# An attention block with rotating score slots: the first metric beside the normalisation, a bank per key block, roots on VectorE, closing work spread wider

## The chip, the cores and the metric

One core of a Trainium2 chip runs the whole kernel. The metric is the device time of one execution in microseconds (us), the median of several; lower is better.

## The reference, cut to what matters

The input is 2048 tokens of width 128; there are 16 heads of width 8.

```python
mod = silu(c) @ wmod                                   # six rows of modulation
h = layernorm(x) * (1 + ca) + sa
v = log_map(mu, h)                                     # clip, roots, arccosh, a scaled direction
q, k, vv = v @ Wq.T, v @ Wk.T, v @ Wv.T
g = abs(eta + 0.1 * tanh(tanh((h - mu) @ W1.T + b1) @ W2.T + b2))    # the metric
at = softmax((q * g) @ k.T / sqrt(8))                  # 16 heads, 2048 x 2048 each
x = x + ga * project(project(mu) + 0.1 * (at @ vv) @ Wo.T)
h = layernorm(x) * (1 + cb) + sb
x = x + gb * ((silu(h @ wg.T) * (h @ wu.T)) @ wd.T)    # hidden width 384
```

The kernel never takes a row maximum of the scores. It subtracts from each query a bound, |q| times the largest |k| of the head, which needs the root of |q|^2 * max|k|^2. It is this root that the change moves.

## The kernel before, in words

The queries are cut into four blocks of 512 (`NB`); Bk numbers them. A block has 64 steps j (`STEPS`): four groups of four heads (`NG`, `GH`) times 16 key tiles of 128. In each step TensorE makes the scores of two heads (`score(.., half_=0)`), then the product of probabilities and values of step j-2 (`product`), then the scores of the other two heads. ScalarE takes the exponential of each half step u = 2j or 2j+1, a tile of 128 x 1024, from PSUM into `probs`. There are 128 of these in a block and 512 in all. The scores of a half step go into one of three slots of two PSUM banks each (`slot_bank`), here slot u % 3. Since 128 is not a multiple of 3, the first half steps of a block fall on slots that the last ones of the block before have just used; the waits on `exped` for u < 3 and the order called `early` in steps 1 and 63 (the product goes ahead of the first score) provide for that. The products gather in bank 6 (`O_bank`), which VectorE copies out after every 16 steps (`evacuate`).

Bank 7 (`M_bank`) serves everything else. In block 0 the list `later` puts the values of the key blocks and the metric, query and norm of query blocks 1 to 3 between the score steps, at the steps that `V_AT`, `M1_AT`, `M2_AT`, `Q_AT`, `NQ_AT` name. In blocks 1 to 3 the closing work of the block before (output projection `t_wo`, second normalisation, `t_transpose`, three `t_gate` and `t_up`, four parts of `t_down`) stands at the steps `AT_WO` to `AT_DOWN`. On VectorE `Tail` does its part.

Before block 0 lies a preamble: normalisation and log map in token order, transposes (`metric_T` for h, `v_T` for v), first metric (`metric1`, `metric2`, with `tanh1`, `tanh2` on ScalarE), keys (`k_of`, two PSUM banks in turns), the first queries, squares and norms of the keys (`nk`, `k_max`), the bound of query block 0 (`bound`), and the splitting of keys and queries into three bf16 parts that go through DRAM to get their layout (`store_k`, `load_k`, `load_q`, `load_shift` in SyncE's queue, in this order). The bounds of query blocks 1 to 3 are three ScalarE roots at step 49 of block 0 (`ROOT_AT`). If a check of the sums fails, every engine runs a second pass (`blocks(1)`) with true maxima.

In SyncE's queue one instruction that waits holds up all behind it. In blocks 1 to 3 the order there is: the gathers of groups 0 and 1 (`gather`, 8 transfers each), the store of the block before (waits for `y_ready`, which `tail.result()` gives after the last `t_down`), the reload of x, the gather of group 2.

Of the kernel before, what the change touches and what calls it, by code (L numbers as in the profile page):

```python
# [56 lines left out]
AT_WO, AT_TR, AT_GATE, AT_UP, AT_DOWN = 8, 15, (19, 24, 29), (22, 27, 32), (37, 39, 41, 43)  # L57
# [3 lines left out]
M1_AT, M2_AT, Q_AT, NQ_AT, ROOT_AT = ((7, 10), (21, 24), (35, 38)), (13, 27, 41), (16, 30, 44), (19, 33, 47), 49  # L61
# [17 lines left out]
def build(nc, x, columns, wmod, fixed, w1t, w2t, w_att, wgt, wut, wdt, spread, out):  # L79
    with ExitStack() as ctx:  # L80
# [27 lines left out]
        hs_bf = sb("hs_bf", [P, H], BF16)  # L108
# [24 lines left out]
        def tmp(words, *shape, dt=F32):  # L133
# [5 lines left out]
            if len(shape) == 2:  # L139
# [10 lines left out]
        shift_f = [O_sb[0:H, 0, :], O_sb[0:H, 3, :], x_res[0:H, :, :].rearrange("p a b -> p (a b)"),  # L150
                   h_tm[0:H, 0:TPB, :].rearrange("p a b -> p (a b)")]
# [58 lines left out]
        names = """c_in wmod_in w_in hs_ready ffn_in const_ready pe_mod mod_ready silu_ready ffn_ready  # L210
# [22 lines left out]
        def ring(j):  # L233

            return j % RING if j < STEPS - 1 else 1
# [140 lines left out]
        def _(pool):  # L376
            pool.memset(half[:, :], 0.5).then_inc(S["const_ready"], 1)
            pool.memset(mhalf[:, :], -0.5).then_inc(S["const_ready"], 1)
            pool.memset(V_op[:, :, :], 1.0).then_inc(S["ones_ready"], 1)
            pool.wait_ge(S["const_ready"], 2)  # L380
# [13 lines left out]
            pool.tensor_copy(hs_bf[:, :], hs_sb).then_inc(S["hs_ready"], 1)  # L394
# [24 lines left out]
        def _(act):  # L419
# [29 lines left out]
            for b in range(NB):  # L449
                copy_hT(b)  # L450
# [4 lines left out]
            act.activation(ln_u, u, ACT.Ln).then_inc(S["ln_out"], 1)  # L455

# [5 lines left out]
            def k_split1(b):  # L462
# [3 lines left out]
                act.activation(k_parts[b][:, 0, :], bank(2 + b % 2), ACT.Identity).then_inc(S["k_hi"], 1)  # L466
                act.activation(sqks[b], bank(2 + b % 2), ACT.Square).then_inc(S["k_sq"], 1)
# [5 lines left out]
            def bound(b):  # L473

                if b == 0:
                    act.wait_ge(S["nq_ps"], 1)
                    act.wait_ge(S["kmax_ready"], 1)
                else:
                    act.wait_ge(S["nq_sb"], b)
                act.activation(shift_f[b], bank(6)[0:H, :] if b == 0 else shift_f[b], ACT.Sqrt,  # L480
                               scale=kmax[0:H, NB:NB + 1]).then_inc(S["bound"], 1)

            for m in range(MH):
                tanh1(0, m)
            copy_vT(0)
            copy_vT(1)
            k_split1(0)
            act.wait_ge(S["cols_ps"], 1)
# [888 lines left out]
```

## Time and profile before

| | us |
|---|---|
| median of 3 runs (598.18 to 598.79) | 598.61 |
| profiled execution, span of its instructions | 599.2 |
| profiled execution, its own time | 601.03 |
| TensorE busy / ScalarE busy in the span | 545.6 / 525.6 |
| VectorE busy / GpSimd busy | 143.9 / 23.0 |

The span runs from the first to the last instruction. The busy time of TensorE is that of matmuls, which overlap one another, so 91% does not mean that it does 91% of what it could. The granted clock of TensorE has two levels, 1.2 and 2.4 GHz; its mean over the span was 0.959 of the higher one.

### The profile page before, as it was taken

Reading aid. Unit: us, or ns where it says so; the run is one execution under the profiler, and the core shown is the slowest. Engines: PE = TensorE matmul, PEld = TensorE weight load, DVE = VectorE, ACT = ScalarE, POOL = GpSimd, SP = SyncE. Lnnn points to the kernel's source line nnn. Section 1 sums busy time; section 2 is a strip of 40 time slices with the busy share of each in tenths; the row PEclk is TensorE's granted clock in tenths of the full one; section 3 lists DMA queues with packets and bytes.
Section 4 is the critical chain, followed back from the end, with each engine's and each line's share of the span. In section 5 each row is a group of like instructions: output and inputs, shape, how many; then the busy total and the mean of one; then the engine's idle time right before and its main releaser. Section 6 shows DMA issues by size and latency. Waiting matters only on the chain.

```text
span 599.2 us, 16356 instructions
## 1 busy us (share of the span) xinstructions
PE 545.6 (91%) x7230; PEld 232.9 (39%) x7230; DVE 143.9 (24%) x407; ACT 525.6 (88%) x596; POOL 23.0 (4%) x25
## 2 busy tenths in 40 slices
PE   1566998999979999999999999999999999999855
PEld 0332543554423343345433333454333334553222
DVE  6963303030310251110000711100005211003063
ACT  3564898999999999999999999999999999999811
POOL 2300100000000010000000100000000000000010
PEclk9576999999989999999999999999999999999978
DMA  6012267010040110000100200001000000010000
GB/s 187 4 35 86 94 158 190 8 33 5 29 107 1 46 48 10 3 10 19 29 2 19 74 10 2 5 7 40 7 7 7 4 8 1 11 55 11 1 0 24
DMA packets 13770, 20.90 MB, mean 35 GB/s; under 512 B 2043, under 2 KB 10363, under 8 KB 13411
## 3 DMA queue, kind: packets, MB, share of 16 engines
q1 hardware_dynamic: 12851, 17.48, 11.4%
q0 software_dynamic: 560, 1.97, 0.9%
q8 instruction: 58, 0.95, 0.7%
q10 hardware_dynamic: 288, 0.40, 0.2%
q14 instruction: 13, 0.11, 0.1%
HBM read 13.41 MB, written 4.19 MB: 29 GB/s over the span
## 4 chain that ended last, share of the span: by engine, by line
PE 62%; ACT 17%; issue 8%; DVE 6%; DMA 4%; SPq 1%; POOL 0%; ACTq 0%; DVEq 0%
PE ps L719 26%; PE ps L736 25%; ACT probs L519 14%; PE ps L655 8%; DMA K_op<-k_scr 3%; DVE probs L969 1%; DMA probs<-x_dram 1%; DMA k_scr<-arena 1%; PE ps L624 1%; ACT arena L531 1%; ACT arena L447 1%; SPq L266 1%; PE ps L564 0%; DVE kmax L1038 0%; DVE arena L958 0%
## 5 line engine op out<-in xcount | busy, mean ns | idle before, releaser
L519 ACT ACTIVATE probs<-ps 128x1024 f32<-128x1024 f32 x512 | 481.3, 1121 | 17.0 <-PE ps L719 15.3
L719 PE MATMUL ps<-Q_op,K_op 73*32 73x512 bf16 x4096 | 291.6, 381 | 11.0 <-ACT probs L519 6.7
L736 PE MATMUL ps<-probs,V_op 128*32 128x512 f32 x2048 | 271.7, 595 | 1.3 <-ACT probs L519 0.8
L719 PEld LDWEIGHTS ps<-Q_op,K_op 73*32 73x32 bf16 x4096 | 117.5, 96 | 238.6 <-issue 124.0
L736 PEld LDWEIGHTS ps<-probs,V_op 128*32 128x32 f32 x2048 | 68.8, 111 | 51.3 <-issue 4.9
L1130 DVE COPY O_sb<-ps 128x512 f32<-128x512 f32 x16 | 11.1, 691 | 153.6 <-PE ps L736 153.6
L385 POOL TENSOR_TENSOR small<-small,half 128x4 f32<-128x4 f32 x4 | 5.5, 1383 | 403.3 <-DVE small L1214 403.3
L571 PE MATMUL ps<-fixed_sb,arena 128*128 128x128 f32 x32 | 7.4, 391 | 14.6 <-POOL arena L391 11.1
L1244 DVE SCALAR_TENSOR_TENSOR arena<-arena,ps 128x512 f32<-128x512 f32 x12 | 8.2, 687 | 46.0 <-ACT arena L537 46.0
L1250 DVE TENSOR_TENSOR arena<-ps,arena 128x512 f32<-128x512 f32 x12 | 8.3, 691 | 40.5 <-PE ps L655 40.4
L1264 DVE TENSOR_TENSOR arena<-ps,arena 128x512 f32<-128x512 f32 x3 | 2.1, 691 | 59.9 <-PE ps L655 59.9
L1015 DVE TENSOR_SCALAR arena<-arena,cols 128x512 f32<-128x512 f32 x4 | 1.9, 484 | 60.2 <-ACT arena L438 60.2
L1170 DVE RECIPROCAL arena<-arena 128x512 f32<-128x512 f32 (+1 forms) x4 | 13.4, 3353 | 0.1
L655 PE MATMUL ps<-wd_f,arena 128*32 128x128 f32 x384 | 13.2, 272 | 0.0
L655 PE MATMUL ps<-Q_op,w_sb 128*32 128x512 f32 x96 | 12.6, 592 | 0.0
L655 PE MATMUL ps<-arena,wg_f 128*32 128x512 f32 x96 | 12.5, 593 | 0.0
L655 PE MATMUL ps<-arena,wu_f 128*32 128x512 f32 x96 | 12.5, 592 | 0.0
L655 PEld LDWEIGHTS ps<-wd_f,arena 128*32 128x32 f32 x384 | 11.6, 109 | 2.2 <-issue 0.6
L690 PE MATMUL ps<-ones_bf 128*128 128x512 bf16 x14 | 6.4, 623 | 6.5 <-POOL small L385 6.5
L531 ACT ACTIVATE arena<-ps,mod_cols 128x512 f32<-128x512 f32 x4 | 3.5, 879 | 10.1 <-PE ps L751 10.1
L571 PEld LDWEIGHTS ps<-fixed_sb,arena 128*128 128x128 f32 x32 | 5.3, 198 | 17.6 <-issue 8.4
L537 ACT ACTIVATE arena<-ps 128x512 f32<-128x512 f32 x12 | 8.0, 670 | 3.4 <-PE ps L655 3.4
(167 smaller groups left out, 237.9 us busy)
## 6 DMA issues: line engine op xcount, KB each, us to landing
K_op<-k_scr SPq DMA_DIRECT2D x16, 288.0 KB
Q_op<-q_scr SPq DMA_DIRECT2D x9, 384.0 KB
arena<-O_sb SPq DMA_DIRECT2D x120, 16.0 KB
q_scr<-arena POOLq DMA_DIRECT2D x3, 384.0 KB, 3.0
probs<-x_dram SPq DMA_DIRECT2D x4, 256.0 KB, 4.8
x_res<-x_dram SPq DMA_DIRECT2D x4, 256.0 KB, 3.2
out_dram<-arena SPq DMA_DIRECT2D x4, 256.0 KB, 2.4
Q_op<-q_scr SPq DMA_DIRECT2D x3, 288.0 KB
```

The lines of the kernel that those rows point to most:

```text
L519: act.activation(probs[:, 2 * ring(j) + half_, :], slot_bank(u % 3), ACT.Exp)\
L531: act.activation(h2_T, M_bank, ACT.Identity, scale=mod_cols[:, 0:1], bias=mod_cols[:, 1:2]).then_inc(S["h2T_done"], 1)
L537: act.activation(th[m], from_bank, ACT.Tanh, scale=0.5).then_inc(S["gate_th"], 1)
L571: ins = pe.transpose(bank(b % 2)[:, P * t:P * (t + 1)], src[:, TPB * b + t, :], ident_sb)
L655: ins = pe.matmul(to[CW * c:CW * (c + 1), :], weights[:, CW * c:CW * (c + 1)], moving, start=start, stop=stop, tile_position=(0, CW * c))
L690: ins = pe.matmul(to, ones_bf[:, 0:P], ones_bf[:, 0:BT], start=True, stop=True)
L719: ins = pe.matmul(slot_bank(u % 3)[CW * c:CW * (c + 1), i, :], K_op[0:rows, kt // TPB, h, at_k:at_k + CW], Q_op[0:rows, at_q:at_q + BT], s ...
L736: ins = pe.matmul(O_bank[32 * i:32 * (i + 1), :], V_op[:, kt, VW * h:VW * h + 32], probs[:, 2 * ring(j) + i // 2, BT * (i % 2):BT * (i % 2 ...
L1130: dve.tensor_copy(O_sb[:, g, :], O_bank).then_inc(S["o_evac"], 1)
L1170: c.did(dve.reciprocal(rec_T[rows, :], rec_T[rows, :]))
L1244: dve.scalar_tensor_tensor(gl[m], th[m], 1.0, gates, ALU.add, ALU.mult).then_inc(S["gated"], 1)
L1250: dve.tensor_tensor(hid[:, m, :], ups, gl[m], ALU.mult).then_inc(S["glu_done"], 1)
```

## The change

It does six things. (1) The first metric is computed while the other blocks are still being normalised; ScalarE's list of table loads changes with it. (2) Each of the four key blocks gets a PSUM bank of its own (2 to 5), the four key norms go into the four quarters of one bank, and one reduction over 128 rows and three small copies replace four reductions. (3) A root of nothing on ScalarE (`kmax[:, 7:8]`) ahead of the keys loads the root table early. (4) The bounds of query blocks 1 to 3 are computed on VectorE, by a shift of the bits and one Newton step; the first instruction reads `M_bank` and gives it free. (5) In the first pass slots and `probs` are counted on through all blocks, `early` is gone, and ScalarE's blocks 1 to 3 are written out instead of looped. (6) The closing work stands further apart. Ten matmuls that only keep TensorE busy are put ahead of the first `v_T`, and ten instead of seven ahead of the scores.

```diff
-AT_WO, AT_TR, AT_GATE, AT_UP, AT_DOWN = 8, 15, (19, 24, 29), (22, 27, 32), (37, 39, 41, 43)
+AT_WO, AT_TR, AT_GATE, AT_UP, AT_DOWN = 8, 15, (19, 27, 35), (23, 31, 39), (43, 47, 51, 55)
...
+        def slot(Bk, p, u):
+            return (u + 2 * STEPS * Bk) % 3 if p == 0 else u % 3
+        def early(p, j):
+            return p == 1 and j in (1, STEPS - 1)
+        def ring(Bk, p, j):
+            if p == 0:
+                return (STEPS * Bk + j) % RING
+            return 1 if j == STEPS - 1 else j % RING
...
+            act.activation(kmax[:, 7:8], half[:, 0:1], ACT.Sqrt)
...
-                    if j == ROOT_AT:
-                        bound(b)
...
-                if u >= 3:
+                if u >= 3 or (p == 0 and not start):
                     pe.wait_ge(S["exped"], Bk * 2 * STEPS + u - 2)
...
+            keep_warm(10, bank(5))
             v_T(0)
...
+            def k_max():
+                dve.wait_ge(S["nk_ps"], NB)
+                dve.tensor_reduce(kmax[:, 0:1], bank(0), AX.X, ALU.max).then_inc(S["nk_done"], 1)
+                dve.wait_ge(S["nk_done"], 1)
+                for b in range(1, NB):
+                    vec.did(dve.tensor_copy(kmax[0:H, b:b + 1], kmax[2 * H * b:2 * H * b + H, 0:1]))
+                vec.after()
+                dve.tensor_reduce(kmax[0:H, NB:NB + 1], kmax[0:H, 0:NB], AX.X, ALU.max).then_inc(S["kmax_ready"], 1)
...
-                dve.tensor_copy(shift_f[b], M_bank[0:H, :]).then_inc(S["nq_sb"], 1)
-
+                dve.tensor_scalar(root_a, M_bank[0:H, :], kmax[0:H, NB:NB + 1], None, ALU.mult).then_inc(S["nq_sb"], 1)
+                if b == NB - 1:
+                    evacuate(0, 2)
+                dve.wait_ge(S["nq_sb"], b)
+                vec.did(dve.tensor_scalar(root_b.bitcast(I32), root_a.bitcast(I32), 1, None,
+                                          ALU.logical_shift_right))
+                vec.after()
+                vec.did(dve.tensor_scalar(root_b.bitcast(I32), root_b.bitcast(I32), 0x1FBD0000, None,
+                                          ALU.add))
+                vec.after()
+                vec.did(dve.reciprocal(shift_f[b], root_b))
...
                     for m in range(NM):
+                        if m == NM - 1:
+                            evacuate(Bk, 1)
                         tail.gated(m, M_bank)
                         tail.glu(m, M_bank)
-                    evacuate(Bk, 1)
+                    evacuate(Bk, 2)
                     tail.result()
-                    evacuate(Bk, 2)
```

TensorE's program at its start, before: from the transposes of h (L571, 16 of them for four blocks) to the norms of the keys. L583 and L596 are the first metric's two products, L624 the keys, L642 the queries, L635 the key norms, L650 the query norm, L690 the matmuls that only keep the engine busy.

```order
L571 MATMUL ps<-fixed_sb,arena 128x128 x16
L583 MATMUL ps<-Q_op,w_sb 128x512 x2
L607 MATMUL ps<-flag_f,mod 128x1 x2
L571 MATMUL ps<-fixed_sb,arena 128x128 x8
L624 MATMUL ps<-arena,w_att_sb 128x512
L596 MATMUL ps<-Q_op,w_sb 128x512 x2
L571 MATMUL ps<-fixed_sb,arena 128x128 x8
L642 MATMUL ps<-arena,w_att_sb 128x512
L624 MATMUL ps<-arena,w_att_sb 128x512 x3
L635 MATMUL ps<-probs,hs_bf 16x512 x4
L650 MATMUL ps<-sqq,hs_bf 16x512
L690 MATMUL ps<-ones_bf 128x512 x7
```

The same stretch after (L594 transposes, L606 and L619 the metric, L685 the ten matmuls, L646 keys, L665 queries):

```order
L594 MATMUL ps<-fixed_sb,arena 128x128 x4
L606 MATMUL ps<-Q_op,w_sb 128x512 x2
L629 MATMUL ps<-flag_f,mod 128x1 x2
L594 MATMUL ps<-fixed_sb,arena 128x128 x4
L619 MATMUL ps<-Q_op,w_sb 128x512 x2
L594 MATMUL ps<-fixed_sb,arena 128x128 x8
L685 MATMUL ps<-ones_bf 128x512 x10
L594 MATMUL ps<-fixed_sb,arena 128x128 x8
L646 MATMUL ps<-arena,w_att_sb 128x512
L665 MATMUL ps<-arena,w_att_sb 128x512
L594 MATMUL ps<-fixed_sb,arena 128x128 x4
L646 MATMUL ps<-arena,w_att_sb 128x512
```

Both products of the metric now stand ahead of the transposes of h blocks 2 and 3, and the queries ahead of three of the four key products.

ScalarE's program at its start, before: the copies of the transposed h (L427), the three roots of the log map (L442), the logarithm (L455), the first tanh (L433).

```order
L427 ACTIVATE Q_op<-ps,cols 128x512 x4
L442 ACTIVATE small<-small 128x16 x3
L455 ACT_TABLE_LOAD
L455 ACTIVATE small<-small 128x16
L433 ACT_TABLE_LOAD
L433 ACTIVATE Q_op<-ps,cols 128x512 x2
L459 ACTIVATE arena<-ps 128x512 x2
```

The same after (L439 copies, L445 and L450 tanh, L454 the three roots, L474 the logarithm, L476 the root of nothing):

```order
L439 ACTIVATE Q_op<-ps,cols 128x512
L445 ACT_TABLE_LOAD
L445 ACTIVATE Q_op<-ps,cols 128x512 x2
L439 ACTIVATE Q_op<-ps,cols 128x512
L466 ACTIVATE mod_cols<-ps 128x2
L450 ACTIVATE arena<-ps,cols 128x512
L439 ACTIVATE Q_op<-ps,cols 128x512 x2
L454 ACT_TABLE_LOAD
L454 ACTIVATE small<-small 128x16 x3
L474 ACT_TABLE_LOAD
L474 ACTIVATE small<-small 128x16
L476 ACT_TABLE_LOAD
```

Two tanh of the first layer, one of the second and two table loads now stand ahead of the three roots.

ScalarE's program at step 49 of block 0, before; after, the last tanh is followed by 74 exponentials in one row (`L538 ACTIVATE probs<-ps 128x1024 x74`).

```order
L438 ACTIVATE arena<-ps,cols 128x512
L519 ACTIVATE probs<-ps 128x1024 x14
L480 ACT_TABLE_LOAD
L480 ACTIVATE O_sb<-O_sb,kmax 16x512
L480 ACTIVATE x_res<-x_res,kmax 16x512
L480 ACTIVATE arena<-arena,kmax 16x512
L519 ACT_TABLE_LOAD
L519 ACTIVATE probs<-ps 128x1024 x28
```

Two table loads and three roots are gone from between the exponentials.

## Rows read from the trace of the kernel before

**Rows 1.** The page: TensorE's granted clock in 40 slices of 15 us, tenths of 2.4 GHz.

```profile
PEclk9576999999989999999999999999999999999978
```

**Rows 2.** Windows preamble, block 0, block 2: length; PE, PEld, DVE, ACT, POOL busy; clock.

```profile
0.00:57.40 57.40, 28.19 (x70) 12.75 (x70) 39.41 (x154) 28.27 (x52) 9.41 (x12) 0.73 0.26 77
57.40:195.80 138.40, 131.43 (x1783) 61.48 (x1787) 24.26 (x56) 129.74 (x142) 4.00 (x5) 0.98 0.26 70
...
319.40:443.00 123.60, 122.53 (x1720) 49.89 (x1716) 20.13 (x48) 121.21 (x133) 2.38 (x2) 1.00 0.08 20
```

**Rows 3.** Timeline of ScalarE in block 2: start, length, line, idle before.

```profile
318.36 2.07 ACT L519 ACTIVATE probs<-ps 128x1024 f32<-128x1024 f32 x2
...
321.99 27.75 ACT L519 ACTIVATE probs<-ps 128x1024 f32<-128x1024 f32 x30 [0.27 <-PE ps L719]
349.47 0.91 ACT L531 ACTIVATE arena<-ps,mod_cols 128x512 f32<-128x512 f32 x1
350.13 7.58 ACT L519 ACTIVATE probs<-ps 128x1024 f32<-128x1024 f32 x8
357.36 0.85 ACT L537 ACTIVATE arena<-ps 128x512 f32<-128x512 f32 x1
357.84 9.73 ACT L519 ACTIVATE probs<-ps 128x1024 f32<-128x1024 f32 x10
...
403.17 3.84 ACT L519 ACTIVATE probs<-ps 128x1024 f32<-128x1024 f32 x4 [0.27 <-PE ps L719]
407.28 36.77 ACT L519 ACTIVATE probs<-ps 128x1024 f32<-128x1024 f32 x40 [0.27 <-PE ps L719]
```

**Rows 4.** Timeline of TensorE in block 2, steps 32 to 34.

```profile
382.59 1.05 PE L655 MATMUL ps<-arena,wu_f 128*32 128x512 f32 x8
383.45 0.63 PE L719 MATMUL ps<-Q_op,K_op 73*32 73x512 bf16 x8
...
386.71 1.07 PE L719 MATMUL ps<-Q_op,K_op 73*32 73x512 bf16 x16
...
388.44 1.07 PE L719 MATMUL ps<-Q_op,K_op 73*32 73x512 bf16 x16
```

**Rows 5.** Timeline of ScalarE about step 49 of block 0.

```profile
164.61 1.28 ACT L480 ACT_TABLE_LOAD   x1
...
169.16 4.69 ACT L519 ACTIVATE probs<-ps 128x1024 f32<-128x1024 f32 x5
174.73 22.11 ACT L519 ACTIVATE probs<-ps 128x1024 f32<-128x1024 f32 x24 [0.88 <-PE ps L719]
```

**Rows 6.** Timeline of ScalarE: first copy of transposed h, first root of the log map.

```profile
19.08 0.67 ACT L427 ACTIVATE Q_op<-ps,cols 128x512 f32<-128x512 f32 x1
...
27.07 0.22 ACT L442 ACTIVATE small<-small 128x16 f32<-128x16 f32 x1 [0.49 <-DVE small L974]
```

**Rows 7.** Timeline of TensorE in the preamble, first half of the metric.

```profile
25.65 2.89 PE L583 MATMUL ps<-Q_op,w_sb 128*128 128x512 f32 x4
```

**Rows 8.** The chain that ended last, end of the preamble.

```profile
48.88 0.69 DVE kmax L1038
...
52.71 1.28 ACT L480
...
55.16 2.17 DMA Q_op<-wmod_sb
```

**Rows 9.** Timeline of SyncE's queue in the preamble.

```profile
44.50 1.13 SPq L287 DMA_DIRECT2D q_scr<-arena  x2
47.87 2.06 SPq L273 DMA_DIRECT2D Q_op<-q_scr  x3
```

**Rows 10.** Timeline of SyncE's queue in block 3, first gather of group 2.

```profile
539.83 0.65 SPq L313 DMA_DIRECT2D arena<-O_sb  x1
```

**Rows 11.** Timeline of VectorE, block 3 and its end.

```profile
547.08 3.35 DVE L1170 RECIPROCAL arena<-arena 96x512 f32<-96x512 f32 x1
...
567.95 0.69 DVE L1130 COPY O_sb<-ps 128x512 f32<-128x512 f32 x1 [16.80 <-PE ps L736]
```

More of the change, by code:

```diff
@@ L448, in _ @@
                                bias=nmr[:, t:t + 1]).then_inc(S["xn_done"], 1)
-            for b in range(NB):
-                copy_hT(b)
+            copy_hT(0)
+            for m in range(MH):
+                tanh1(0, m)
+            copy_hT(1)
+            act.wait_ge(S["cols_ps"], 1)
+            act.activation(mod_cols[:, :], M_bank[:, 0:2], ACT.Identity).then_inc(S["cols_sb"], 1)
+            tanh2(0)
+            copy_hT(2)
+            copy_hT(3)
             root(y0, a2, 2)
@@ L539, in blocks @@
             def blocks(p):
-                block_steps(NB * p, False)
-                with act.Fori(NB * p + 1, NB * (p + 1)) as Bk:
-                    block_steps(Bk, True)
+                block_steps(NB * p, False, p)
+                if p == 0:
+                    for Bk in range(1, NB):
+                        block_steps(Bk, True, p)
+                else:
+                    with act.Fori(NB * p + 1, NB * (p + 1)) as Bk:
+                        block_steps(Bk, True, p)
                 last = NB * (p + 1) - 1
@@ L599, in metric2 @@
                 ins.then_inc(S["m2_ps"], 1)
[L601 to L602 removed]
+            metric_T(0)
             for m in range(MH):
@@ L649, in nq @@
                 pe.wait_ge(S["q_f"], b + 1)
-                pe.matmul((M_bank if b else bank(6))[0:H, :], hs_bf[:, :], sqq[:, :], start=True, stop=True)\
+                pe.matmul((M_bank if b else bank(6))[0:H, :], hs_bf[:, 0:H], sqq[:, :], start=True, stop=True)\
                     .then_inc(S["nq_ps"], 1)
@@ L657, in by_columns, with keep_warm @@
                 return ins
+            def keep_warm(n, to):
+                for _ in range(n):
+                    ins = pe.matmul(to, ones_bf[:, 0:P], ones_bf[:, 0:BT], start=True, stop=True)
+                ins.then_inc(S["warm"], 1)
+            keep_warm(10, bank(5))
             v_T(0)
@@ L685, in later @@
                         nq(b)
-            def keep_warm(n, to):
-                for _ in range(n):
-                    ins = pe.matmul(to, ones_bf[:, 0:P], ones_bf[:, 0:BT], start=True, stop=True)
-                ins.then_inc(S["warm"], 1)
             def score(Bk, j, p, half_):
@@ L776, in block_steps @@
                 for j in range(STEPS):
-                    early = j in (1, STEPS - 1)
-                    if not early:
+                    if not early(p, j):
                         score(Bk, j, p, 0)
                     if j >= 2:
-                        product(Bk, j - 2)
+                        product(Bk, p, j - 2)
                     elif tails:
-                        product(Bk - 1, STEPS + j - 2)
-                    if early:
+                        product(Bk - 1, p, STEPS + j - 2)
+                    if early(p, j):
                         score(Bk, j, p, 0)
@@ L817, in blocks @@
                         block_steps(Bk, True, p)
-                product(last, STEPS - 2)
-                product(last, STEPS - 1)
+                product(last, p, STEPS - 2)
+                product(last, p, STEPS - 1)
                 pe.wait_ge(S["o_evac"], NG * (last + 1))
@@ L974, in _, with metric @@
             dve.tensor_scalar(a2, n2, 1.0, EPS, ALU.add, ALU.add).then_inc(S["root_in"], 1)
+            def metric(b):
+                vec.after()
+                dve.wait_ge(S["m2_sb"], b + 1)
+                vec.did(dve.tensor_scalar(g_fm[:, b, :], g_fm[:, b, :], 0.1 * DH ** -0.5, eta_s, ALU.mult, ALU.add))
+            metric(0)
             dve.wait_ge(S["root_out"], 2)
@@ L1009, in _ @@
                 ins.then_inc(S["v_ready"], 1)
-            def metric(b):
-                vec.after()
-                dve.wait_ge(S["m2_sb"], b + 1)
-                vec.did(dve.tensor_scalar(g_fm[:, b, :], g_fm[:, b, :], 0.1 * DH ** -0.5, eta_s, ALU.mult, ALU.add))
             def queries(b):
@@ L1141, in _ @@
                 queries_norm(b)
-            evacuate(0, 2)
-            for b in range(1, NB):
                 shift(b)
```

155 lines of the change are left out of this document (79 added, 76 removed).

## The prediction

> **What bounds the kernel now.** I read the windows first, to cut the span into stages: preamble 57.4 us, block 0 138.4 us, blocks 1 to 3 near 123.6 us each (370.8), and so 599.2 - 57.4 - 138.4 - 370.8 = 32.6 us behind them [rows 2]. In the blocks TensorE and ScalarE are both busy nearly all the time, so the busy shares do not decide; the timelines do. ScalarE's own pace: eight exponentials from 350.13 to 357.36, 7.23 us or 0.904 each, 1.81 a step [rows 3]. TensorE's own pace without other work: from 386.71 to 388.44, 1.73 a step [rows 4]. Left alone ScalarE is the bound, by 0.08 us a step. TensorE's extra work makes it the bound for a while: the `t_up` from 382.59 holds back the next score to 383.45, 0.86 us [rows 4]; two steps with one `t_down` each take 407.28 - 403.17 = 4.11 us instead of 3.45, so a `t_down` costs 0.66 [rows 3].
>
> What an undisturbed block would take by ScalarE: 128 x 0.904 = 115.7, the copy of h2 0.66 (349.47 to 350.13) and three gates of 0.48 (357.36 to 357.84), 117.8 us [rows 3]. It takes 123.6 [rows 2]. So 5.8 us a block are lost, and the question for each edit is how many of them it gives back.
>
> **Slots counted on (boundaries).** From the last exponential of block 1 at 318.36 to the third of block 2 at 321.99, three starts on, 3.63 us pass where 2.71 are ScalarE's pace: 0.92 lost. The 40 exponentials from 407.28, across steps 44.5 to 64, take 36.77 us where 39 x 0.904 and a last one of 1.02 make 36.28: 0.49 lost, of which 0.14 is the first start counted above, so 0.35 belongs to the turned order in step 63 [rows 3]. About 1.27 us for each of the boundaries into blocks 2 and 3; I take 1.05 for the one into block 1 (its step 63 is less tight) and 0.35 at the end of block 3, together 3.9. With a third slot at the boundary it is like any other step, in which ScalarE sees no wait. What the edit adds is one wait, u = 0 on the exponential three before, met by then. Bounds: 3 (the copy out of bank 6, 0.69 us [rows 11], now shows a little) to 4.2.
>
> **Closing work wider.** Every extra piece costs what exceeds TensorE's lead. After `t_down` at step 43 ScalarE sets the pace again; with the last at 55, twelve more steps run at 1.73 instead of 1.81: 12 x 0.08 = 0.97 a block. Against it, the third copy out of bank 6 (steps 49, 50) now falls where no lead is left; it delays the product by some 0.2 to 0.3, estimated from the 0.69 copy against the 0.86 of two half scores that stand between [rows 4, 11]. 0.67 a block, 2.0 in all, between 1.0 and 2.9. The work itself is the same.
>
> What is queued behind: `y_ready` comes 12 steps later, and behind it in SyncE's queue the gather of group 2. It matters in block 3, where the normalisation stands ahead of the last copy. Before, first gather 539.83, reciprocal from 547.08 for 3.35 us, and about 0.7 more, end near 551.2: 11.3 us [rows 10, 11]. Now it starts with step 56 plus 0.4 plus three transfers' issue of about 0.5 each (0.65 for one [rows 10]), so it is over near 0.4 + 1.5 + 11.3 = 13.2 us behind the start of step 56. The last copy starts at 567.95 [rows 11], 1.35 behind the end of the blocks at 566.6, and so 8 x 1.81 + 1.35 = 15.8 behind the start of step 56. Hidden, by 2.6 us.
>
> **Roots of blocks 1 to 3 off ScalarE.** Between 164.61 and 169.16 ScalarE does two table loads and three roots: 4.55 us. TensorE runs dry, its clock falls (the 8 in the twelfth slice [rows 1]), and the five exponentials from 169.16 are followed only at 174.73, 5.57 us where 4.52 are due: 1.05 [rows 5]. Sum 5.6; TensorE's chance to get ahead in between is worth nothing, since three slots are all its lead. VectorE gets instead, three times, a reciprocal of 3.35 and seven light instructions of at most 0.69 each, at most 8.2 us [rows 11]. It is busy 24 of 138 us in block 0 [rows 2], the first instruction frees bank 7 as the copy did, and for the last of them `evacuate(0, 2)` stands in the middle. Taken at 0; were the cover gone, 8 us of one of them at most.
>
> The Trainium skill (ScalarE: Activation LUTs, What ACT_TABLE_LOAD costs) counts a drain of 1.38 us on top of each load's 1.28. The trace shows 1.28 [rows 5] and the next instruction right behind; by the page the roots would give back 2.8 more, and the loads of the preamble below take 1.4 more.
>
> **Preamble.** Here one edit costs and one gains. The cost: ScalarE now runs two tanh, the metric's second tanh and two loads ahead of the first root, which starts at 27.07 now [rows 6]. At half clock a pass of the metric's products takes 0.85 (25.65, four passes at mostly half clock, 2.89 [rows 7]). From 19.8 (first h copied [rows 6]): four passes 3.4, tanh 0.7 (sized by the copies of 0.67 [rows 6]), the next four passes at full clock 1.7 or half 3.4, tanh 0.7, two copies, together 1.3, and a load of 1.28, with the small products and transposes between, near 1 us: first root at 29.6 to 31.7, so 2.6 to 4.6 late. I take 2.6, since TensorE, which idled between transposes, now works on from 19.8 and the clock should rise. The whole log map, and v, is late by as much.
>
> The gain: the four key norms went through one bank, each waiting for the reduction of the last: from the second reduction at 48.88 to 52.71 two more rounds and a small closing one take 3.8 us. At 52.71 the root table is loaded, 1.28, before the bound [rows 8]. With a bank each and one reduction, the bound is ready near 50 instead of 54.7, in spite of the late log map. But the first score waits for a transfer: `load_shift`, issued 55.16, landed 2.17 later [rows 8]. Ahead of it in the queue stand the last q store (issue up to 45.6) and, 2.24 behind, three `load_q` of 0.69 [rows 9]. The q stores wait behind the first key load, that for the key parts, which come 3 to 4 us later now. I get the last q store at 47.7 to 49.1, `load_q` from 50.2 to 51.7, the shift at 52.3 to 53.8, and the first score at 54.6 to 56.1 instead of 57.4. Gain 1.3 to 2.8; since a later first score also meets a lower clock, I take 1.8. Both ends: +3.5 (clock up early and at the first scores), and -1.5 (metric at half clock throughout, first score at 58 or later). The keep-warm matmuls fill waits.
>
> **Sum.** 1.8 + 5.6 + 3.9 + 2.0 = 13.3 us. The profiled execution took 601.0 and would take 587.7; it was 2.4 above the median of 598.6, and against that it is 585.3. The 32.6 us behind the blocks stay.
>
> **Rivals.**
> 1. *The preamble gives nothing or takes.* For it: the instructions and loads put ahead of the root, and a clock whose mean is 0.5 to 0.7 in slices two to four [rows 1]. Against it: the serial rounds really go. 585.3 + 1.8 + 1.5 = 588.6; with it, boundaries at their low end, 589.5.
> 2. *Spreading is a wash and the blocks stay bound in bursts.* 0.86 us come every four steps, which earn 0.32. For it: the work is the same and a stall of 0.5 per piece remains. Then only roots, boundaries and preamble count: 587.3.
> 3. *All at their good ends:* clock up early, 3.5 + 6 + 4.2 + 2.9 = 16.6, 582.0.
> 4. *The gathers of block 3 come late.* If they land 4 us later than now, the 2.6 are used up and 1.4 are lost: 586.7. It decides only from 16 us on.
> 5. *Slower: the second pass is taken.* The bit-shifted root is rough. If one Newton step left it so low that a sum overflowed, or so high that one vanished, all engines would run four more blocks at about 123.6 and 32.6 behind: 527 more, near 1112. Against it: one Newton step from a guess off by a few per cent ends above the root by a few tenths of a per cent, and the bound has 0.8% and a headroom of 48 in it.
> 6. *The written-out exponentials run slower than the looped ones.* Block 0 was written out before, and 24 of them there took 22.11 us, 0.91 each [rows 5]. To matter they would need 13.3 / 384 = 0.035 more each, which that row excludes.
>
> **How the numbers follow.** Forecast (584 to 587) 0.48, rival 1 0.18, rival 2 0.12, rival 3 0.12, rival 4 0.04, slower by 5, 6 or a wait that I don't see 0.03, and 0.03 for something that eats nearly all. 0.2% is 1.2 us, about what a measurement of this kernel can tell from no change. Every case but the last two is faster by more: 0.94 faster; of the last case I give 0.02 to the same and 0.01 to slower: 0.02 same, 0.04 slower. Range: from rival 3 (582.0) to just beyond rival 1's worse end (589.8).
>
> **What the next profile would show.** Exponentials 0.904 apart through all boundaries; no table load in block 0, and no dip of the clock there; blocks 1 to 3 near 121.7; in blocks waits of ScalarE up to step 56 and none behind; the first root of the log map near 29.6 and the first score between 54.6 and 56.1. The prediction is wrong if the first root comes after 32, if a wait for VectorE's long root chain shows in block 0, or if the normalisation in block 3 ends behind the last product.

## The result

| us | before | changed |
|---|---|---|
| median (runs of this comparison, range) | 598.70 (598.18 to 601.13) | 590.10 (589.17 to 592.49) |
| span of the profiled execution | 599.2 | 588.4 |
| its own time | 601.03 | 590.57 |

The ratio is 0.9855, with a 95% interval of 0.9814 to 0.9895: 1.5% faster, by 8.6 us where 13.3 were forecast, and 0.3 us above the upper end of the range. The two profiled executions differ by 10.5 in their own time and by 10.8 in their spans; the one of before was 2.4 us above the median of its kernel.

Windows of the changed kernel, cut as [rows 2]: preamble, block 0, block 2, and what lies behind the blocks.

```profile
0.00:58.00 58.00, 28.41 (x83) 13.67 (x83) 37.32 (x153) 30.31 (x55) 9.46 (x13) 0.80 0.26 77
58.00:189.00 131.00, 130.18 (x1783) 60.91 (x1787) 42.19 (x74) 123.94 (x137) 4.00 (x5) 0.99 0.27 73
...
311.20:433.00 121.80, 121.62 (x1721) 53.20 (x1716) 20.14 (x48) 120.52 (x133) 2.39 (x2) 1.00 0.08 20
...
555.20:588.40 33.20, 18.38 (x233) 9.01 (x233) 15.46 (x50) 4.14 (x7) 2.38 (x2) 0.83 0.04 11
```

The preamble has become 0.6 us longer, block 0 7.4 shorter, block 2 1.8 shorter. VectorE works 18 us more in block 0 (42.19 against 24.26), and nobody waits for it. The page's row of clocks, against [rows 1]:

```profile
PEclk9578899999999999999999999999999999999978
```

The dip to 8 in the twelfth slice is gone. ScalarE's timeline of the changed kernel, across step 49 of block 0 and the boundary at 189.39 (first row), across the output projection of block 1 (second), and across the boundary into block 2 at 311.56 (third), against [rows 3, 5]:

```profile
151.37 49.60 ACT L538 ACTIVATE probs<-ps 128x1024 f32<-128x1024 f32 x54
...
193.95 25.49 ACT L538 ACTIVATE probs<-ps 128x1024 f32<-128x1024 f32 x27
...
307.04 34.28 ACT L538 ACTIVATE probs<-ps 128x1024 f32<-128x1024 f32 x37
```

(The rows are cut where the windows asked for begin and end, so the first two overlap. A row is broken by a gap of more than 0.15 us; smaller losses are found only by counting.) In the first row are 54 exponentials without a break, where two table loads and three roots stood. 53 x 0.904 and a last one of 1.02 make 48.93: 0.67 is lost in 27 steps. The second row loses more than it seems to: 26 x 0.904 + 1.02 = 24.52, so 0.97 is lost in 27 exponentials; the 30 exponentials at the same place in block 2 of before lost 27.75 - 27.24 = 0.51 [rows 3]. That is part of the answer to where the boundary's gain went.

The timeline of TensorE in the preamble (L606 and L619 are the metric's two products), then that of ScalarE:

```profile
17.08 1.09 PE L594 MATMUL ps<-fixed_sb,arena 128*128 128x128 f32 x4 [6.79 <-POOL arena L403]
19.74 3.78 PE L606 MATMUL ps<-Q_op,w_sb 128*128 128x512 f32 x4 [1.58 <-ACT Q_op L439]
23.45 1.01 PE L629 MATMUL ps<-flag_f,mod 1*128 1x1 f32 x4
24.39 1.12 PE L594 MATMUL ps<-fixed_sb,arena 128*128 128x128 f32 x4
25.30 3.08 PE L619 MATMUL ps<-Q_op,w_sb 128*128 128x512 f32 x4
28.22 1.04 PE L594 MATMUL ps<-fixed_sb,arena 128*128 128x128 f32 x8
```

```profile
28.42 0.69 ACT L450 ACTIVATE arena<-ps,cols 128x512 f32<-128x512 f32 x1 [2.13 <-PE ps L619]
29.01 1.26 ACT L439 ACTIVATE Q_op<-ps,cols 128x512 f32<-128x512 f32 x2
30.28 1.28 ACT L454 ACT_TABLE_LOAD   x1
31.58 0.22 ACT L454 ACTIVATE small<-small 128x16 f32<-128x16 f32 x1
```

TensorE has no gap from 19.74 on, yet four transposes still take 1.12 at 24.39, and eight take only 1.04 at 28.22: the records put the rise of the clock at 27.71. In the kernel before, where TensorE idled between the transposes, they put it at 27.67, so closing the gaps did not bring it forward here. So both products of the metric ran almost wholly at half clock, ScalarE waited 2.13 us for the second, and then came the table load. The first root starts at 31.58 instead of 27.07 [rows 6], 4.5 late. Next the queue and the chain that ended last, against [rows 8, 9]:

```profile
42.12 5.37 SPq L273 DMA_DIRECT2D k_scr<-arena  x3
47.53 0.43 SPq L298 DMA_DIRECT2D q_scr<-arena  x1
48.89 0.83 SPq L277 DMA_DIRECT2D K_op<-k_scr  x1
49.77 0.98 SPq L298 DMA_DIRECT2D q_scr<-arena  x2
53.55 2.06 SPq L284 DMA_DIRECT2D Q_op<-q_scr  x3
55.66 0.60 SPq L293 DMA_DIRECT2D Q_op<-wmod_sb  x1
```

```profile
50.32 3.21 DMA q_scr<-arena
53.55 0.69 SPq L284
...
55.66 2.25 DMA Q_op<-wmod_sb
58.05 1.90 PE ps L745 x15
```

The bound itself is ready at 51.07, 3.6 us earlier than before (54.68). So the gain that the new banks were to bring did come, but the bound isn't waited for any more: the chain now runs through two q stores issued behind the first key load, 3.2 us for the last of them to land, three loads and the shift transfer.

### The profile page after: what moved, and what is told of

Its sections match the earlier page's. It is cut to its first block, busy times and chain, and to the rows that moved or that the text cites. A ratio compares the mean times of both kernels' runs of the same rounds, so it can differ in the third digit from the quotient of the medians.

```text
span 588.4 us, 15999 instructions
## 1 busy us (share of the span) xinstructions
PE 542.3 (92%) x7243; PEld 243.6 (41%) x7243; DVE 159.8 (27%) x424; ACT 520.8 (89%) x594; POOL 23.0 (4%) x26
## 3 DMA queue, kind: packets, MB, share of 16 engines
q1 hardware_dynamic: 12851, 17.48, 11.5%
q0 software_dynamic: 560, 1.97, 1.0%
## 4 chain that ended last, share of the span: by engine, by line
PE 74%; ACT 14%; DMA 5%; DVE 4%; SPq 1%; issue 1%; POOL 0%; DVEq 0%
PE ps L745 31%; PE ps L762 30%; ACT probs L538 12%; PE ps L678 8%; DMA K_op<-k_scr 2%; ACT arena L459 1%; DMA k_scr<-arena 1%; DMA probs<-x_dram 1%; SPq L284 1%; PE ps L594 1%; SPq L277 1%; PE ps L606 1%; DMA q_scr<-arena 1%; PE ps L685 1%; PE ps L587 1%
## 5 line engine op out<-in xcount | busy, mean ns | idle before, releaser
L538 ACT ACTIVATE probs<-ps 128x1024 f32<-128x1024 f32 x512 | 479.1, 1132 | 15.3 <-PE ps L745 13.6
L745 PEld LDWEIGHTS ps<-Q_op,K_op 73*32 73x32 bf16 x4096 | 124.6, 96 | 224.2 <-issue 125.5
L762 PEld LDWEIGHTS ps<-probs,V_op 128*32 128x32 f32 x2048 | 71.5, 110 | 48.2 <-ACT probs L538 5.9
L594 PE MATMUL ps<-fixed_sb,arena 128*128 128x128 f32 x32 | 6.4, 351 | 12.5 <-POOL arena L403 6.8
L685 PE MATMUL ps<-ones_bf 128*128 128x512 bf16 x27 | 8.0, 445 | 6.5 <-POOL small L397 6.5
L594 PEld LDWEIGHTS ps<-fixed_sb,arena 128*128 128x128 f32 x32 | 4.9, 179 | 16.1 <-issue 9.9
```

What stands on the lines that cost most here:

```text
L538: act.activation(probs[:, 2 * ring(Bk, p, j) + half_, :], slot_bank(slot(Bk, p, u)), ACT.Exp)\
L594: ins = pe.transpose(bank(b % 2)[:, P * t:P * (t + 1)], src[:, TPB * b + t, :], ident_sb)
L685: ins = pe.matmul(to, ones_bf[:, 0:P], ones_bf[:, 0:BT], start=True, stop=True)
L745: ins = pe.matmul(slot_bank(slot(Bk, p, u))[CW * c:CW * (c + 1), i, :], K_op[0:rows, kt // TPB, h, at_k:at_k + CW], Q_op[0:rows, at_q:at_q ...
L762: ins = pe.matmul(O_bank[32 * i:32 * (i + 1), :], V_op[:, kt, VW * h:VW * h + 32], probs[:, 2 * ring(Bk, p, j) + i // 2, BT * (i % 2):BT * ...
```

## The experiments

The fixed points used below come from the trace of each kernel's profiled execution. A block starts with its first exponential; the fifth column has the times from one start to the next. "Step 16" is what ScalarE loses in steps 16 to 19 of block 0 against its pace of 0.904 an exponential. In the five kernels with 0.35 to 0.38 there TensorE doesn't wait for key tiles in these steps; in the others it does, for the tiles loaded last, between 0.36 us (e2) and 1.71 (before).

| kernel | median us | ratio (95% interval) | first score | block 0 to 1, 1 to 2, 2 to 3 | step 16 |
|---|---|---|---|---|---|
| before | 598.70 | | 57.46 | 137.69, 123.59, 123.63 | 2.26 |
| changed | 590.10 | 0.9855 (0.9814 to 0.9895) | 58.05 | 130.25, 122.17, 121.87 | 0.98 |
| e1_slots | 597.68 | 0.9963 (0.9938 to 0.9987) | 57.66 | 137.02, 122.62, 122.85 | 1.00 |
| e2_roots | 594.46 | 0.9897 (0.9860 to 0.9934) | 57.65 | 130.69, 123.63, 123.62 | 0.91 |
| e3_spread | 596.42 | 0.9936 (0.9915 to 0.9956) | 57.92 | 136.74, 122.59, 122.60 | 0.35 |
| e4_old_preamble | 589.68 | 0.9825 (0.9791 to 0.9858) | 55.11 | 131.56, 122.13, 121.84 | 1.69 |
| e5_changed_again | 590.45 | 0.9841 (0.9821 to 0.9861) | 59.12 | 129.67, 122.11, 121.87 | 0.37 |
| e6_q_stores_first | 588.43 | 0.9804 (0.9781 to 0.9827) | 53.87 | 132.30, 122.11, 121.87 | 1.78 |
| e7_metric_late | 588.28 | 0.9813 (0.9793 to 0.9834) | 54.69 | 129.89, 122.16, 121.88 | 0.38 |
| e8_late_and_q_first | 585.47 | 0.9779 (0.9749 to 0.9810) | 51.76 | 130.52, 122.13, 121.87 | 1.21 |
| e9_warm_start | 589.39 | 0.9830 (0.9810 to 0.9850) | 55.20 | 131.22, 122.17, 121.87 | 1.92 |
| e10_closing_later | 590.01 | 0.9850 (0.9828 to 0.9872) | 52.47 | 131.29, 123.09, 122.71 | 2.00 |
| e11_no_first_ten | 586.37 | 0.9783 (0.9767 to 0.9800) | 53.55 | 129.65, 122.12, 121.84 | 0.37 |
| e12_late_and_q_again | 584.81 | 0.9758 (0.9739 to 0.9776) | 52.16 | 129.65, 122.13, 121.84 | 0.38 |

The kernel before ran beside each group: 599.71 (e1 to e4), 600.03 (e5 to e8), 599.85 (e9 to e12). Blocks repeat within 0.1 us between kernels that share them; "step 16" does not, and it is in block 0's length. Nor does the first score repeat: before, e1 to e3 and e4 have the same preamble, and it comes at 57.5 to 57.9 in the first four and at 55.11 in e4, where the clock was up from 36.61 to 53.68 and so the rounds of the key norms ran fast. A difference of 2 us in one trace of the preamble can be the clock alone; the medians have to agree with it.

**The parts alone.** Three kernels put one edit each into the kernel before. First the slots:

```diff
+        def slot(Bk, p, u):
+            return (u + 2 * STEPS * Bk) % 3 if p == 0 else u % 3
...
-                if u >= 3:
+                if u >= 3 or (p == 0 and not start):
...
-                    if early:
+                    if early(p, j):
...
```

The rest of this edit carries the new slot numbers through and writes ScalarE's blocks 1 to 3 out.

> The kernel before with the slots and probs counted on through the blocks (and ScalarE's blocks written out), nothing else. My theory, that the parts inside the blocks gave what the prediction said and that the shortfall lies in the preamble: 3.9 us less, between 3 and 4.2, all of it at the block boundaries; the preamble as before. The rival, that the edits inside the blocks are worth less apart than the sum said: under 2.5 us.

Measured: 597.68, 2.0 us less by the medians (0.8 to 3.7 by the interval), so they alone would have fitted the rival as well. ScalarE's timeline about the boundary into block 2 (at 317.96):

```profile
308.92 39.09 ACT L529 ACTIVATE probs<-ps 128x1024 f32<-128x1024 f32 x42
```

The boundary itself has no break any more, against the 0.92 lost there in [rows 3]. But 41 x 0.904 + 1.02 = 38.08, so 1.0 is lost in this row. The starts of its exponentials put 0.79 of it at step 9, where the output projection is (0.62 in block 1, 0.79 in block 3); before, 0.35 was lost there. In the changed kernel it is 0.80 in block 1 and 0.57 in blocks 2 and 3. Blocks 1, 2 and 3 are shorter by 0.97, 0.78 and 0.61, block 0 by about 0.27 at its end: 2.6 us by trace, and not 3.9.

The roots:

```diff
-                    if j == ROOT_AT:
-                        bound(b)
...
-                dve.tensor_copy(shift_f[b], M_bank[0:H, :]).then_inc(S["nq_sb"], 1)
+                dve.tensor_scalar(root_a, M_bank[0:H, :], kmax[0:H, NB:NB + 1], None, ALU.mult).then_inc(S["nq_sb"], 1)
+                if b == NB - 1:
+                    evacuate(0, 2)
...
```

> The kernel before with the roots of query blocks 1 to 3 moved to VectorE, nothing else. My theory: 5.6 us less; the two table loads, the three roots and the dip of TensorE's clock at step 49 go. The rival, that TensorE used the pause to get ahead or that VectorE's longer chain costs something: 3 to 4.5 us less.

Measured: 594.46, 5.3 less by the medians. The timeline of ScalarE from the last tanh on, across step 49:

```profile
150.50 39.52 ACT L518 ACTIVATE probs<-ps 128x1024 f32<-128x1024 f32 x43
```

Waits, loads and roots in steps 49 to 63 of block 0 fall from 6.02 to 0.36 us: 5.66, as forecast (5.6). Block 0 as a whole is 7.0 shorter; the other 1.35 are at step 16, where the roots have no part. Blocks 1 to 3 are as before. VectorE's chain is hidden. The price of the roots is not fixed, though: in e1 and e3, which still have them, the clock was low for 6.8 us behind step 49 and not for 3.4, and steps 49 to 57 lost 6.8 and 6.9 us where the trace of before lost 5.9. So 5.66 is nearer the low end of what the edit saves.

The spread:

```diff
-AT_WO, AT_TR, AT_GATE, AT_UP, AT_DOWN = 8, 15, (19, 24, 29), (22, 27, 32), (37, 39, 41, 43)
+AT_WO, AT_TR, AT_GATE, AT_UP, AT_DOWN = 8, 15, (19, 27, 35), (23, 31, 39), (43, 47, 51, 55)
...
                     for m in range(NM):
+                        if m == NM - 1:
+                            evacuate(Bk, 1)
                         tail.gated(m, M_bank)
                         tail.glu(m, M_bank)
-                    evacuate(Bk, 1)
+                    evacuate(Bk, 2)
                     tail.result()
-                    evacuate(Bk, 2)
```

> The kernel before with the closing work and VectorE's copies at their new places, nothing else. My theory: 2.0 us less, between 1.0 and 2.9, 0.67 in each of blocks 1 to 3. The rival, that spreading is a wash since every piece still exceeds what four steps earn: 0 to 0.5 us.

Measured: 596.42, 3.3 less by the medians. Blocks 1 to 3 are shorter by 1.00, 1.03 and 1.04, together 3.1 where 2.0 were forecast. But not all of it is lost beside the closing work. From step 19 to step 60, 5.6 us a block are lost before and 4.9 in e3, so 0.7 is gained there. The other 0.32 lies at step 62: 0.34 was lost there before, in front of the turned order of step 63, and 0.02 in e3. The slots counted on remove this same loss, so the two edits overlap by it. Between the exponentials of steps 49 to 51 the third copy shows as a wait of 0.06, not 0.2 to 0.3. By trace the three parts make 2.6 + 5.66 + 3.1 = 11.4, where the sum on record had 11.5; the changed kernel has 10.9 of it, for the overlap counts once.

**The preamble.** e4_old_preamble is the changed kernel with the whole preamble of before:

```diff
-            copy_hT(0)
-            for m in range(MH):
-                tanh1(0, m)
-            copy_hT(1)
...
+            for b in range(NB):
+                copy_hT(b)
...
-                dve.tensor_reduce(kmax[:, 0:1], bank(0), AX.X, ALU.max).then_inc(S["nk_done"], 1)
+                dve.tensor_reduce(kmax[0:H, b:b + 1], bank(0)[0:H, :], AX.X, ALU.max).then_inc(S["nk_done"], 1)
```

> The three edits inside the blocks together, with the preamble of before: no metric beside the normalisation, no bank per key block, no root of nothing. My theory: the parts add, 11.0 to 11.5 us less than before, so 587.2 to 587.7, and faster than the full change by 0.6 us (by the traces) to 3 us (by the medians): the new preamble costs. The rival, that the new preamble is worth something and the blocks' parts overlap: slower than the full change, 591 or more.

Measured: 589.68, 10.0 below the kernel before it ran beside; 11.0 to 11.5 were expected, which its median misses by 1 us. Still that is all of the change's gain, so the new preamble gives nothing by the medians; whether it takes a few tenths is inside the intervals (0.9825 against 0.9855 and 0.9841). The next four kernels ran together and ask why.

> The changed kernel once more, so that the variants of its preamble that follow can be compared on the same chip. 590 us; first exponential near 59 us; the blocks as in its first trace.

The changed kernel a second time, without an edit: 590.45, the root at 32.02, the clock up at 28.67. So the root was late in two executions out of two.

In e6_q_stores_first the first key load is issued behind all three q stores:

```diff
-                if n == 0:
+                if n == 2:
                     sp.wait_ge(k_st[0], 16 * PARTS)
                     load_k(0, 0, K_first[0])
```

> The changed kernel with one transfer moved in SyncE's queue: the load of the first keys goes behind the three stores of the query parts instead of between the first and the second. Theory Q, that the changed preamble ends in SyncE's queue (q stores held behind the wait of the first key load, bound ready 6 us before): the last q store goes out at about 48.2 instead of 50.3, the first score comes 2 to 3 us earlier, 587 to 588. Rival, that the key load or the late log map decides: under 0.7 us.

In e7_metric_late the first metric is again behind the normalisation and the roots, on three engines; banks, reduction and the queries' place ahead of the transposes of v blocks 2 and 3 stay as changed (ahead of three of the four key products they stood in the kernel before, too):

```diff
-            copy_hT(0)
-            for m in range(MH):
-                tanh1(0, m)
-            copy_hT(1)
...
-            tanh2(0)
-            copy_hT(2)
-            copy_hT(3)
+            for b in range(NB):
+                copy_hT(b)
...
+            for m in range(MH):
+                tanh1(0, m)
...
             k_square(0)
             k_high(0)
+            tanh2(0)
...
```

> The changed kernel with the first metric back behind the normalisation (the table of the root of nothing is loaded behind the second tanh); banks, norms, queue and blocks as in the change. Theory L, that the metric ahead of the roots makes the log map 4.5 us late and that this is what ate the gain: first root at 27.1 instead of 31.6, first score 2.5 to 4 us earlier, 586 to 588. Rival, that the work only moves (two tanh, a table load and products come back behind the log map) and the clock is lower: within 1 us of the changed kernel.

e8_late_and_q_first has both edits.

> Both edits. If L and Q both hold they should mostly add, since the one moves when the parts are ready and the other what the queue does with them: first score near 53, 5 us earlier, 585. If only Q holds, as the run with the q stores first; if only L, as the run with the late metric.

Measured: 588.43, 588.28 and 585.47, against 590.45 for the changed kernel beside them: 2.0, 2.2 and 5.0 less. The first two end a little above the 587 to 588 and 586 to 588 expected, the third near its 585, and the two edits add. SyncE's queue in e6, e7 and e8:

```profile
45.76 1.43 SPq L298 DMA_DIRECT2D q_scr<-arena  x3
47.23 0.83 SPq L277 DMA_DIRECT2D K_op<-k_scr  x1
48.59 2.04 SPq L284 DMA_DIRECT2D Q_op<-q_scr  x3
```

```profile
45.25 0.83 SPq L277 DMA_DIRECT2D K_op<-k_scr  x1
46.13 0.98 SPq L298 DMA_DIRECT2D q_scr<-arena  x2
49.95 2.06 SPq L284 DMA_DIRECT2D Q_op<-q_scr  x3
```

```profile
43.84 1.42 SPq L298 DMA_DIRECT2D q_scr<-arena  x3
45.30 0.83 SPq L277 DMA_DIRECT2D K_op<-k_scr  x1
46.66 2.04 SPq L284 DMA_DIRECT2D Q_op<-q_scr  x3
```

With the key load ahead, the last q store is issued at 46.68 and `load_q` follows 3.27 later; behind the stores, it follows 1.9 later (46.73 and 48.59 in e6). Two things are told apart by counting each point from the first root of the log map (the last two columns are distances from it):

| us | first root | `load_q` behind it | first score behind it |
|---|---|---|---|
| before | 27.07 | 20.80 | 30.39 |
| changed / e5 | 31.58 / 32.02 | 21.97 / 22.31 | 26.47 / 27.10 |
| e6 (q stores first) | 29.39 | 19.20 | 24.48 |
| e7 (metric late) | 27.01 | 22.94 | 27.68 |
| e8 (both) | 26.95 | 19.71 | 24.81 |

The order of the queue is worth 2 to 3 us of the way from the root to the first score; the place of the metric is worth 4.5 to 5 us of the root itself. In e6 the root came at 29.39 because the clock rose at 22.95 in that execution; nothing in its edit touches that. e6's first score of 53.87 therefore says more than its edit is worth, and its median, over five executions, is the better witness.

To see how much of the late root is the clock, e9_warm_start puts 26 matmuls on idle banks between the modulation and the first transposes of the changed kernel:

```diff
             ins.then_inc(S["pe_mod"], 1)
+            keep_warm(26, bank(5))
```

> The changed kernel with 26 more matmuls that only keep TensorE busy, between the modulation's product and the first transposes, where it idles for 6.8 us. Nothing else. Theory C, that half of the lateness of the first root is the clock, which in the changed kernel is at its lower level for the metric's first product and most of the second: with the clock up from the start the first root comes near 29.4 instead of 31.6 to 32.0, and the first score some 2 us earlier, 588 to 589. Rival, that ScalarE's order and table load alone decide: first root still after 31. If the clock is low when the 26 begin, they take twice as long and push the first transposes back.

TensorE and ScalarE in e9:

```profile
10.13 6.59 PE L594 MATMUL ps<-ones_bf 128*128 128x512 bf16 x26
17.13 0.63 PE L602 MATMUL ps<-fixed_sb,arena 128*128 128x128 f32 x4 [0.41 <-POOL arena L403]
19.79 1.98 PE L614 MATMUL ps<-Q_op,w_sb 128*128 128x512 f32 x4 [2.04 <-ACT Q_op L439]
...
22.73 1.88 PE L627 MATMUL ps<-Q_op,w_sb 128*128 128x512 f32 x4
```

```profile
26.51 1.28 ACT L454 ACT_TABLE_LOAD   x1
27.81 0.22 ACT L454 ACTIVATE small<-small 128x16 f32<-128x16 f32 x1
```

Each product takes 1.9 to 2.0 instead of 3.8 and 3.1, and the root comes at 27.81, 3.8 earlier than in the changed kernel and hardly later than before the change. It was expected at 29.4. So nearly the whole lateness of the root is the half clock; ScalarE's extra work and its table load, which are all still there, leave 0.7 of it. The first score, 55.20, is 2.9 us earlier than in the changed kernel and 3.9 earlier than in e5. But the median, 589.39, is only 0.7 and 1.1 lower (e5 ran on another occasion, so the ratios are the better comparison: 0.983 against 0.9855 and 0.9841, which overlap). In the profiled execution step 16 takes back 0.9 and 1.6 of it. How much the early matmuls are worth in the end is not resolved.

**Could the closing work gain more?** The wait at the output projection looked like a lead that TensorE had not yet made up by step 8. e10_closing_later moves all closing work of e8 two steps back:

```diff
-AT_WO, AT_TR, AT_GATE, AT_UP, AT_DOWN = 8, 15, (19, 27, 35), (23, 31, 39), (43, 47, 51, 55)
+AT_WO, AT_TR, AT_GATE, AT_UP, AT_DOWN = 10, 17, (21, 29, 37), (25, 33, 41), (45, 49, 53, 57)
```

> The kernel with late metric and q stores first (585.5), with all closing work two steps later: output projection at step 10, the last down at 57. Theory W, that the waits at step 9 have grown from 0.35 to 0.6 to 0.85 us a block because TensorE has no longer made up its lead by step 8: two steps later they fall by 0.16 a block and two more steps run at TensorE's pace, 0.16, so 0.3 a block, 0.9 us in all, blocks 1 to 3 at 121.8, 121.6 and 120.7. Rival, that the projection waits for the normalisation: then the waits at its step go to 0.35 at once. If the lead is at its limit anyway: no change.

Measured: 590.01, 5.2 slower than the same kernel without the edit (e12, beside it), where 0.9 less was expected. The spans of the two traces differ by 4.3: blocks 1 to 3 are longer by 0.96, 0.87 and 0.82, together 2.7, and step 16, which the edit doesn't touch, has 1.6 more (2.00 against 0.38). So about 2.7 us are the edit's. The waits at the projection stay what they were, now at step 11: the idea falls. A new loss of 1.7 us comes at step 34 of each block; the block as a whole loses about half of that. Timelines of TensorE, VectorE and ScalarE in block 1 of e10, steps 32 to 34 (L673 is `t_up(1)`, L1289 `glu(1)`, L1171 the copy out of bank 6, L758 the product):

```profile
247.61 1.05 PE L673 MATMUL ps<-arena,wu_f 128*32 128x512 f32 x8
248.47 0.62 PE L741 MATMUL ps<-Q_op,K_op 73*32 73x512 bf16 x8
250.25 1.07 PE L758 MATMUL ps<-probs,V_op 128*32 128x512 f32 x8 [1.15 <-ACT probs L536]
```

```profile
248.81 0.69 DVE L1289 TENSOR_TENSOR arena<-ps,arena 128x512 f32<-128x512 f32 x1 [6.18 <-PE ps L673]
249.42 0.68 DVE L1171 COPY O_sb<-ps 128x512 f32<-128x512 f32 x1
```

```profile
251.78 6.52 ACT L536 ACTIVATE probs<-ps 128x1024 f32<-128x1024 f32 x7 [1.61 <-PE ps L741]
```

With `t_up(1)` at step 33 instead of 31, `evacuate(Bk, 1)` stands on VectorE behind `glu(1)`, which waits for `t_up(1)`. The product that opens a new group (step 34) needs bank 6 and starts at 250.25, 0.15 behind the copy's end; the profile names the probabilities as its releaser, but those of step 32, which it reads, were ready at 247.41. ScalarE then waits 1.61. In the change `t_up(1)` is at step 31, and VectorE is free for 2.3 us before the copy can begin; two steps later, 3.6 us, is too late. Why the wait at the projection grew with the slots counted on, from 0.35 to 0.80 and 0.57 in the changed kernel, stays open; it isn't the normalisation, which in block 1 of the changed kernel ends at 204.10, 0.5 before the projection starts.

**The ten matmuls.** e11_no_first_ten is e8 without the matmuls ahead of the first `v_T`:

```diff
-            keep_warm(10, bank(5))
             v_T(0)
```

> The kernel with late metric and q stores first, without the ten matmuls ahead of the first transposes of v. If they hold the clock up for the keys and queries, it falls before step 36 of the time axis without them and the first score comes 1 to 2 us later; if they fill an idle time that decides nothing, within 0.3 us.

> The kernel with late metric and q stores first once more, as the comparison for the two runs before it on the same chip and as a second measurement of the version that beat both kernels: 585.5, 2.2% under the kernel before.

e12_late_and_q_again is e8 once more, beside it: 584.81, and 586.37 without the ten (the intervals of the ratios, 0.9739 to 0.9776 and 0.9767 to 0.9800, just touch). In e12 eight transposes at 32.60 take 1.44 us and two products of `k_of(0)` 1.13; without the ten the transposes take 1.97 at 32.50 and the products 2.08, as at half clock in the kernel before. The first score is 1.4 later. One trace against one would not show this, for in e11 the small products at 29.12, ahead of where the two programs part, already take 1.01 us against 0.60. But the same transposes take 1.44 in all four kernels with the late metric and the ten (e7, e8, e10, e12) and 1.9 to 2.0 in all six without the ten (before, e1 to e4, e11). So this piece is worth about 1.5 us once the log map is early enough for it. In the changed kernel itself it isn't: there TensorE idles for 5.67 us behind the ten, and the transposes take 1.97 at 37.09. e12 and e8, 584.8 and 585.5, are the best version: 2.2 to 2.4% below the kernel before, and e8 0.8% below the changed kernel beside it (e5).

## Why the prediction was right or wrong

- **Which way, and the blocks' sum: right.** From first to last exponential the profiled executions differ by 12.2 us (507.5 to 495.3), of which 1.3 is step 16; 10.9 are left for the 11.5 forecast. No table load is left in block 0, no dip of the clock, and no break at a boundary, as the text wanted to see.
- **Roots off ScalarE: right,** in mechanism and size (5.66 for 5.6). The load is 1.28 with the next instruction right behind also in the changed preamble (30.28, 31.58), so the further 2.8 us by the drain in the Trainium skill (ScalarE: Activation LUTs, What ACT_TABLE_LOAD costs) did not come.
- **Slots counted on: right mechanism, size off** (3.9; by e1 2.6). The step took a boundary in isolation. The break is gone in full (1.30 between steps 62 and 1 for the 1.27 forecast), but a part comes back as a longer wait at the output projection, some eight steps later: 0.27 to 0.44 a block in e1, 0.45 and twice 0.22 in the changed kernel. The low bound of 3 was too high as well.
- **Closing work wider: right mechanism, and the net size right partly by luck** (0.67 a block; steps 19 to 60 gain 0.68 in the changed kernel and 0.7 in e3). The deduction for the third copy out of bank 6, 0.2 to 0.3 a block, measured 0.06, so the wider spacing itself gave some 0.75 and not the 0.97 it was put at; the two errors cancel. The 3.1 of e3 alone has another 0.32 a block from step 62, which the prediction had rightly put under the boundaries. Rival 2, a wash, is out.
- **Gathers of block 3: right.** The normalisation there ends at 555.04 and the last copy starts at 556.78: 1.7 hidden, for the 2.6 forecast.
- **Preamble: the step that failed.** "I take 2.6, since TensorE … works on from 19.8 and the clock should rise" took the good end of 29.6 to 31.7 (the terms as listed add up to 29.9 there); the root came at 31.58, since the clock rose only at 27.7, when the second product was nearly done. What failed is the reason: work without gaps did not bring the clock up earlier than before. e9, with the clock up from 11.77, has the root at 27.81, and e7, with the metric behind it, at 27.01. By the sign that the text set itself, a first root after 32, the first execution just passes and e5, at 32.02, doesn't. Way and root together: the sum implied a first score 25.9 us behind a root at 29.7. It came 26.5 behind a root at 31.6. So 1.9 of the 2.4 us missed are the root's, and 0.6 the queue's: `load_q` came 2.80 behind the end of the last q store's issue (50.75 to 53.55), where I had put 2.24. The path through the queue was forecast rightly; why its last piece was longer stays open, but without the key load ahead it is 1.40 (e6, e8). First score 58.05 for 54.6 to 56.1: an end the text had named (58 or later), but with too little weight. In place of +1.8 the step measured -0.6 at the first score and -1.0 at the first exponential, for the first scores ran at half clock (sixteen matmuls in 1.90 us, 1.05 before).
- **Behind the blocks: 0.4 missed.** The stage "stays" by the sum; from the last exponential's start it is 33.6 before and 34.0 after. In the twelve other kernels it is 33.8 to 34.6, so this may be no more than the spread of single executions.
- **The sum.** By the traces: -1.0 for the preamble, 5.7 for the roots, 5.2 for slots and spread together (5.9 forecast), 1.3 for step 16, -0.4 behind the blocks, together 10.8, the difference of the spans. The 1.3 is luck: the prediction had no such term, and step 16 has anything from 0.35 to 2.26 in kernels whose edits don't touch it. The medians differ by 8.6, and by about 9.6 against the later runs of before (599.7 to 600.0); what lies between that and 10.8 is that the profiled execution of before lay above the median of its kernel. Rival 1 (588.6 to 589.5) was the nearest case, for the reason it named: the instructions and loads put ahead of the root, and the clock.

## What to carry to other kernels

Before side work is put ahead of the head of a serial chain, price it at the slow clock: what it costs is the chain's delay, and here the clock did not rise earlier for the gaps being closed (27.71 against 27.67). In a queue that serves in order, look for the transfer whose data everything waits for and ask which big load stands ahead of it: moving one load behind three stores gave 2 us. When work is spread, every copy that frees a shared accumulator must stay ahead of work that waits; moving the work two steps too far cost 2.7 us. And when two edits are priced apart, ask whether they remove the same wait: here 0.3 us a block was in both.

## What the runs showed of the hardware

- TensorE without a gap from 19.74 on was granted the higher clock at 27.71 in one execution, at 28.67 in another, and in a third (e6), with the same program up to there, at 22.95. The durations tell the same: four transposes take 1.1 us at the lower and 0.6 at the higher clock. With 26 matmuls ahead the clock was up from 11.77 to 32.25.
- TensorE's wait at step 16 of block 0, for key tiles still in transfer, was between nothing (e3, e5, e7, e11, e12) and 1.71 us (before); ScalarE lost 0.35 to 2.26 us with it. For the same program it was 0.38 (e12) and 1.21 (e8). It doesn't follow the first score: before, with one of the latest (57.46), lost most, and e12, with one of the earliest (52.16), nearly least. Why it varies stays open.
- With the first key load ahead of it, the last q store took 3.21 us to land in the changed kernel and `load_q` followed its issue by 3.3 us (e7 too); in e6 and e8, with the key load behind the stores, by 1.9.
